# Two-step sorting with a turn across lanes in the planner of a max-plus layer

## The reference, cut to what matters

```
for a block of tokens xx:                      # all 16384 tokens
    t = max over d of (xx[:, d] + Wt[f, d])    # 256 d, 1024 f  -> t[token, f]
    z = t + bt; piecewise linear functions of z, mixed with gelu(x Wc) by a sigmoid gate, times Wd
```

## Time and profile before

| | |
|---|---|
| time, median of 3 runs (lowest, highest) | 6708.94 us (6705.71, 6711.29) |
| the profiled execution: time; span from its first to its last instruction | 6724.72 us; 6722.9 us |
| mean granted TensorE clock of the profiled execution | 0.959 of full speed |
| busy over the span: TensorE matmul, VectorE, ScalarE, GpSimd | 5978.2, 5148.0, 3296.8, 1789.5 us |

### The profile page before, as it was taken

The page is one execution under the profiler, slowest core; times in us unless marked ns, Lnnn a source line. Parts: engine busy times, 40 slices in busy tenths (PEclk is TensorE's granted clock), DMA queues, the critical chain, the costliest instruction groups (busy, mean ns, idle before and its releaser), DMA issues. The chain is left out here.

```text
span 6722.9 us, 104063 instructions
## 1 busy us (share of the span) xinstructions
PE 5978.2 (89%) x29554; PEld 4157.6 (62%) x29554; DVE 5148.0 (77%) x9496; ACT 3296.8 (49%) x6081; POOL 1789.5 (27%) x3698
## 2 busy tenths in 40 slices
PE   9998999999988884699999996876675999999999
PEld 6667999999977773466666664544443444444444
DVE  8993333333358888799999998998785999999998
ACT  6662222222234442466666664221122877787777
POOL 3330000000014442465656564247463000000000
PEclk9999999999989997899999998998887999999999
DMA  4440000000024442222121221246354222212221
GB/s 137 134 131 18 0 0 0 0 0 0 0 81 151 154 154 94 82 71 75 70 75 70 75 73 57 67 142 221 136 199 159 67 82 79 79 67 81 77 80 49
DMA packets 366380, 552.30 MB, mean 82 GB/s; under 512 B 29264, under 2 KB 299216, under 8 KB 366288
## 3 DMA queue, kind: packets, MB, share of 16 engines
q1 hardware_dynamic: 322944, 400.58, 18.2%
q0 software_dynamic: 43344, 150.64, 6.6%
HBM read 310.46 MB, written 240.67 MB: 82 GB/s over the span
## 5 line engine op out<-in xcount | busy, mean ns | idle before, releaser
L1710 PE MATMUL t_fetched<-t_wpart,t_onehot 128*128 128x512 f32 x4096 | 1221.6, 420 | 35.7 <-DVE t_tout L1815 15.5
L1815 DVE SCALAR_TENSOR_TENSOR t_tout<-t_fetched,t_top,t_tout 128x1024 f32<-128x1024 f32 x896 | 1149.3, 1283 | 35.5 <-PE t_fetched L1710 4.5
L580 PEld LDWEIGHTS l_ps<-hx,l_whh 128*128 128x128 f32 x8192 | 962.7, 193 | 16.8 <-DVE hx L521 3.7
L580 PE MATMUL l_ps<-hx,l_whh 128*128 (+1 forms) x8192 | 950.7, 275 | 3.2 <-DVE hx L521 3.2
L1710 PEld LDWEIGHTS t_fetched<-t_wpart,t_onehot 128*128 128x128 f32 x4096 | 690.7, 188 | 269.4 <-DVE t_tout L1815 131.0
L2112 PE MATMUL ts_fetched<-t_wpart,ts_onehot 128*128 128x512 f32 x2008 | 632.7, 450 | 209.2 <-ACT ts_onehot L2087 82.4
L545 ACT ACTIVATE l_act<-l_ps 128x128 f32<-128x128 f32 x1024 | 283.6, 277 | 1055.0 <-PE l_ps L580 1055.0
L2606 DVE SCALAR_TENSOR_TENSOR f_line<-f_hinge,f_vec,f_line 128x1024 f32<-128x1024 f32 x512 | 656.8, 1283 | 50.6 <-ACT f_hinge L2490 36.2
L2112 PEld LDWEIGHTS ts_fetched<-t_wpart,ts_onehot 128*128 128x128 f32 x2008 | 380.8, 207 | 397.8 <-DVE ts_tout L2180 232.6
L512 DVE TENSOR_TENSOR l_ig<-l_act 128x128 f32<-128x128 f32 x256 | 74.8, 292 | 592.3 <-ACT l_act L545 592.3
L2540 PE MATMUL f_pso<-f_fused,f_wd 128*128 128x512 f32 x1024 | 469.6, 602 | 36.8 <-DVE f_fused L2593 36.8
(11 more groups left out here) (379 smaller groups left out, 10666.6 us busy)
## 6 DMA issues: line engine op xcount, KB each, us to landing
t<-t_tout SPq DMA_DIRECT2D x128, 512.0 KB, 2.6
f_t<-t SPq DMA_DIRECT2D x64, 1024.0 KB, 5.2
g_adj<-in_adj SPq DMA_DIRECT2D x128, 256.0 KB, 3.0
g_adjt<-in_adjt SPq DMA_DIRECT2D x128, 256.0 KB, 2.8
t_x<-x_normalised SPq DMA_DIRECT2D x130, 128.0 KB, 2.3
g_x<-in_x SPq DMA_DIRECT2D x64, 256.0 KB, 2.8
x_kept<-g_x SPq DMA_DIRECT2D x64, 256.0 KB, 2.2
g_x<-x_kept SPq DMA_DIRECT2D x64, 256.0 KB, 2.8
```

The lines of the kernel that those rows point to most:

```text
L580: mm = pe.matmul(ps_g[s][q][:, c2, r, :], w_hh[:, k, row:row + P], hx[:, k, ds(t, 1), :].rearrange("p o b -> p (o b)"), start=False, stop= ...
L1710: mm = pe.matmul(fetched[c % RING][:, h * CH:(h + 1) * CH], one_hot[g][:, c % GRP * P:(c % GRP + 1) * P], w_part[part][:, k, h * CH:(h + 1 ...
L1815: dve.scalar_tensor_tensor(t_out[j][:, :], column[:, :], value, t_out[j][:, :], ALU.add, ALU.max)\
```

## The change

`tropical_plan` alone is changed. (1) The key holds the token's full number: 32768 x open + token + 1, where token + 1 = 128 x (tile + 1) + lane - 127. (2) Each lane sorts its two lists as before, in 16 rounds. (3) TensorE then multiplies the sorted keys with 32 stretches of a doubled identity matrix: the keys of rank r go to the lane that lies 4 x (r mod 32) places further round. In each matmul 8 columns move (four ranks of two halves). (4) VectorE copies the result out of PSUM, counts `above` from it as before, and sorts a second time in 16 rounds. (5) The row number is now read from the key, and the spare rows from a small table, so that a few instructions that made it from tile and lane go.

```diff
+OPEN_ONE = 32768.0
+TURNS = 32
...
         @block.tensor
         def _(pe):
+            pe.wait_ge(ident2_ready, 1)
+            pe.wait_ge(lanes_sorted, 1)
+            by_turn = [t[:, :, :].rearrange("p k (r m) -> p m k r", m=TURNS) for t in (sorted_key, ps_turned)]
+            for m in range(TURNS):
+                mm = pe.matmul(by_turn[1][:, m, :, :], ident2[:, m * (P // TURNS):m * (P // TURNS) + P],
+                               by_turn[0][:, m, :, :], start=True, stop=True)
+            mm.then_inc(lanes_turned, 1)
             pe.wait_ge(counted, 1)
...
+            def descending(src, between):
+                for r in range(TILES // 8):
+                    eight = slice(8 * r, 8 * r + 8)
+                    for k in range(KD):
+                        last = dve.max(sorted_key[:, k, eight], src[:, k, :])
+                    then(last)
+                    for k in range(KD):
+                        last = dve.match_replace(left_key[:, k, :], sorted_key[:, k, eight], src[:, k, :], -1.0)
+                    then(last)
+                    src = left_key
+                    if r == 0:
+                        between()
+
+            def turnable():
+                for r in range(2):
+                    last = dve.tensor_copy(ident2[:, r * P:(r + 1) * P], ident[:, :])
+                last.then_inc(ident2_ready, 1)
+                for r in range(3):
+                    last = dve.tensor_scalar(spare_row[:, r:r + 1], v["p_plus"][:, :], float(TOK + r * P + 1), None, ALU.add)
+                then(last)
...
+            dve.tensor_scalar(token_no[:, :], v["tile_no"][:, 0:TILES], float(P), v["p_plus"][:, :], ALU.mult, ALU.add)
             then(dve.tensor_scalar(key[:, :, :], done_count[:, :].rearrange("p (s k) -> p k s", k=KD),
-                                   -2.0 * P, 2.0 * P * P, ALU.mult, ALU.add))
+                                   -OPEN_ONE, OPEN_ONE * P - (P - 1), ALU.mult, ALU.add))
...
+            descending(key, turnable)
+            dve.sem_inc(lanes_sorted, 1)
+
+            dve.wait_ge(lanes_turned, 1)
+            then(dve.tensor_copy(key[:, :, :], ps_turned[:, :, :]))
             for c, g in enumerate(CLASSES[1:] + (0, CLASSES[0])):
-                last = dve.tensor_scalar(above[:, KD * c:KD * c + KD, :], key[:, :, :], 2.0 * P * (g + 1), None, ALU.is_ge)
+                last = dve.tensor_scalar(above[:, KD * c:KD * c + KD, :], key[:, :, :], OPEN_ONE * (g + 1), None, ALU.is_ge)
             then(last)
             dve.tensor_reduce(count[:, :], above[:, :, :], AX.X, ALU.add).then_inc(counted, 1)
-
-            src = key
...
+            descending(key, find_most)
...
-            dve.tensor_scalar(row[:, :, :], order[:, :, :], -1.0, float(P), ALU.add, ALU.mult)
+            dve.tensor_scalar(no_token[:, :, :], order[:, :, :], 0.0, spare_row[:, 0:1], ALU.is_equal, ALU.mult)
...
-            then(dve.tensor_scalar(row[:, :, :], row[:, :, :], v["p_plus"][:, :], None, ALU.add))
-            then(dve.tensor_tensor(from_row[:, :, :], row[:, :, :], no_token[:, :, :], ALU.add))
-            then(dve.tensor_tensor(row[:, :, :], row[:, :, :], no_token2[:, :, :], ALU.add))
+            dve.scalar_tensor_tensor(from_row[:, :, :], order[:, :, :], -1.0, no_token[:, :, :], ALU.add, ALU.add)
+            then(dve.scalar_tensor_tensor(row[:, :, :], order[:, :, :], -1.0, no_token2[:, :, :], ALU.add, ALU.add))
```

More of the change, by code:

```diff
@@ L1871, in tropical_plan @@
         ps_most = ctx.enter_context(nc.psum_tensor("tp_psmost", [1, C], F32))
+        ps_turned = ctx.enter_context(nc.psum_tensor("tp_psturned", [P, KD, TILES], F32))
         done_count, rows, ident = (v[n] for n in ("done_count", "rows", "ident"))
@@ L1874, in tropical_plan @@
             sem(n) for n in ("counted", "count_turned", "most_ready", "most_turned"))
+        ident2_ready, lanes_sorted, lanes_turned = (sem(n) for n in ("ident2_ready", "lanes_sorted", "lanes_turned"))
         steps = Steps(sem("steps"), 1)
@@ new lines, in turnable, with find_most @@
+            def turnable():
[5 more added lines that the diff above has]
+                then(last)
+            def find_most():
+                dve.wait_ge(count_turned, 1)
+                dve.tensor_reduce(most[:, :], ps_count[:, :], AX.X, ALU.max).then_inc(most_ready, 1)
@@ L1891, in _ @@
             steps.begin(0)
+            dve.tensor_scalar(token_no[:, :], v["tile_no"][:, 0:TILES], float(P), v["p_plus"][:, :], ALU.mult, ALU.add)
             then(dve.tensor_scalar(key[:, :, :], done_count[:, :].rearrange("p (s k) -> p k s", k=KD),
-                                   -2.0 * P, 2.0 * P * P, ALU.mult, ALU.add))
+                                   -OPEN_ONE, OPEN_ONE * P - (P - 1), ALU.mult, ALU.add))
             for k in range(KD):
-                last = dve.tensor_tensor(key[:, k, :], key[:, k, :], v["tile_no"][:, 0:TILES], ALU.add)
+                last = dve.tensor_tensor(key[:, k, :], key[:, k, :], token_no[:, :], ALU.add)
@@ L1917, in _ @@
-            then(dve.tensor_scalar(whole[:, :, :], sorted_key[:, :, :], 0.5 / P, -0.25, ALU.mult, ALU.add))
+            descending(key, find_most)
+            then(dve.tensor_scalar(whole[:, :, :], sorted_key[:, :, :], 1.0 / OPEN_ONE, -0.25, ALU.mult, ALU.add))
             then(dve.tensor_scalar(whole[:, :, :], whole[:, :, :], ROUND, None, ALU.add))
             then(dve.tensor_scalar(whole[:, :, :], whole[:, :, :], ROUND, None, ALU.subtract))
-            dve.tensor_scalar(is_open[:, :, :], sorted_key[:, :, :], 2.0 * P, None, ALU.is_ge)
@@ L1921, in _ @@
-            then(dve.scalar_tensor_tensor(whole[:, :, :], whole[:, :, :], -2.0 * P, sorted_key[:, :, :], ALU.mult, ALU.add))
+            dve.tensor_scalar(is_open[:, :, :], sorted_key[:, :, :], OPEN_ONE, None, ALU.is_ge)
+            then(dve.scalar_tensor_tensor(whole[:, :, :], whole[:, :, :], -OPEN_ONE, sorted_key[:, :, :], ALU.mult, ALU.add))
             then(dve.memset(order[:, :, TILES:SLOTS], 0.0))
             then(dve.tensor_tensor(order[:, :, 0:TILES], whole[:, :, :], is_open[:, :, :], ALU.mult))
-            dve.tensor_scalar(row[:, :, :], order[:, :, :], -1.0, float(P), ALU.add, ALU.mult)
+            dve.tensor_scalar(no_token[:, :, :], order[:, :, :], 0.0, spare_row[:, 0:1], ALU.is_equal, ALU.mult)
@@ L1932, in _ @@
-            then(dve.tensor_tensor(from_row[:, :, :], row[:, :, :], no_token[:, :, :], ALU.add))
-            then(dve.tensor_tensor(row[:, :, :], row[:, :, :], no_token2[:, :, :], ALU.add))
+                last = dve.tensor_scalar(no_token2[:, :, :].rearrange("p k (s r) -> p (k s) r", r=2)[:, :, r],
+                                         order[:, :, :].rearrange("p k (s r) -> p (k s) r", r=2)[:, :, r],
+                                         0.0, spare_row[:, 1 + r:2 + r], ALU.is_equal, ALU.mult)
```

5 lines of the change are left out of this document (1 added, 4 removed).

## The result

| | before | after |
|---|---|---|
| time, median of 4 runs beside each other | 6709.6 us (6705.71 to 6711.29) | 6601.5 us (6599.79 to 6602.89) |
| profiled execution, its own time | 6724.7 us | 6602.1 us |
| ratio, 95% interval | | 0.984 (0.9828 to 0.9853) |

The account below looks back on a forecast made before the run. VectorE bounds the plan and sets the pace in slots of 16 to 3; no engine is full over all slots. Plan +27.5 and slots -162.0 give -134.5 us, so 6708.9 becomes 6574 us, range 6558 to 6598.

Parts of the forecast that it names:

- The start of each half stays: Slots stage: the start of each half costs the same as before; no term in the sum.
- the other stages ... see the same data: Outside plan and slots: only those two can move, the other stages and the 44 us general round see the same data.
- the turn: Plan: 32 float32 matmuls on TensorE, fully exposed, 32 x 0.22 + 0.4 = +7.4 us, bounds 3.8 and 13.4.
- The number of slots: Slots: host calculation of turned lists gives 106 slots and 402 uses instead of 128 and 502, saving 162.0 us.
- The price of a slot: Slots: prices stay, from 22.95 us for 16 candidates to 4.65 us for 2.
- The rest of the plan: Plan: sort +18.9, small copies and adds +1.0, PSUM copy +0.9, row numbers -0.7; whole plan +27.5 us (19 to 36).
- each saved slot only relieves GpSimd's queue: Slots: each slot left out takes its three indirect DMAs off GpSimd's queue, so nothing is put behind anything.
- The gathers: Slots of 2, 3, 4: repeated places stretch DMA by f; 4% for 6598 to 6695 us, 1% no change, 2% slower.
- 273 f - 416: Slots of 2, 3, 4: extra us if DMA time stretches by f; eats the 134.5 us saving at f = 2.0.
- rival 2: Slots: lists don't shrink, so the plan's +27.5 us stands alone, 6736 us; chance 3%.
- the balance was not near perfect: Slots: judges a rival where slots follow the means over lanes, saving 246 us, so 6490 us; chance 2%.
- The rule on small matmuls: Plan: by the skill's some 25 ns a matmul the 32 would take 0.8 us; the forecast preferred the trace's weight loads.

Follow-up runs that it names:

- Experiment 2: Changed kernel with all 32 matmuls on the identity's first 128 columns, so no key leaves its lane: 6754.1 us, 1.0067 of the kernel before.
- experiment 1: Kernel before, unedited, run again; its profile is the second profile of before: 6708.3 us, 1.0001, profiled at 6713.6.
- experiment 11: Kernel before with 128 one-element VectorE memsets ahead of the plan, on the chip where before took 6723.3 us: 6724.9 us, 1.0004.
- experiment 9: Changed kernel with keys split into two fp32r parts moved by one matmul, plus 23 memsets, first chip: 6600.5 us, 0.9816 of the kernel before.
- experiment 10: Changed kernel with keys in two fp32r parts and 23 memsets, run on a second chip: 6589.2 us, 0.982 of the kernel before.
- experiment 13: Changed kernel with 74 matmuls of the identity on TensorE ahead of the turn: 6614.6 us, 0.9839 of the kernel before.
- experiment 5: Changed kernel with ten more slots of 2, on spare rows, in each half: 6682.6 us, 0.9958 of the kernel before.
- experiment 12: Changed kernel with 4 turns instead of 32, four matmuls of 64 columns: 6623.0 us, 0.9853 of the kernel before.
- experiment 4: Kernel before with 101 one-element VectorE memsets ahead of the plan: 6723.4 us, 1.0022 of the kernel before.
- experiment 6: Changed kernel with 26 VectorE memsets ahead of the plan: 6593.2 us, 0.9824 of the kernel before.
- experiment 7: Changed kernel with 64 VectorE memsets ahead of the plan: 6609.0 us, 0.9849 of the kernel before.
- experiment 15: Changed kernel with 26 VectorE memsets again, on a chip where the kernel before takes 6710.5 us: 6594.7 us, 0.9828.
- experiment 3: Kernel before with 32 extra TensorE matmuls behind the plan's transposes: 6708.4 us, 0.9999 of the kernel before.

## Why the prediction was right in kind and 26 us off in size

The steps that failed: "The start of each half stays" (12.5 us), "the other stages ... see the same data" (8.0 us), both terms put at nothing, and the turn at 7.4 us instead of 13.8 (6.4 us). Any one of them is more than the 3.5 us by which the time left the range. By the prediction's own steps, with the misses against 134.5:

- **The number of slots**: right in all twelve classes (x402, 106, 72, 14). Experiment 2 shows that the turn and nothing else of the change brings the saving. The host's calculation, tied to the twelve numbers of before, was the step that carried the forecast.
- **The price of a slot**: held within 2% from 16 down to 3, where VectorE sets the pace. In the class of 2 the forecast took 4.65 us from a profile that held pauses (experiments 1 and 11). Since only 6 of those slots went, this costs less than 2 us. The slots as a whole gave 165.8 instead of 162.0, -3.8 on the miss.
- **The turn**: the step "32 matmuls ... 32 x 0.22 + 0.4 = +7.4" is the mis-sized term. It took 13.79 us, above the upper bound of 13.4, because each float32 call is two instructions; experiments 9 and 10 show it from the other side, with 32 instructions in 6.97 us. The duration of one was right, at the clock of 0.50 that the turn had (experiment 13). The evidence stood in the rows I quoted: L1131 has x16, and the source behind it calls 8. I read them as 16 calls. +6.4.
- **The rest of the plan**: second sort 18.9 for 18.9, copy 0.42 for a share of 0.9; with the turn set aside the plan came 0.5 us under the forecast. The recorded lower bound of 19 us for the plan is too low: its terms' own lower bounds add to 22.7.
- **"The start of each half stays"**, and the claim that each saved slot only relieves GpSimd's queue: wrong. The forecast had a cost for each slot and none for the end of a block. The two gaps with drains in them grew by 12.5 us in the marks (6.3 + 6.2). Experiments 2, 5 and 12 tie their length to the number of slots alone, with turned and unturned lists, and old and new code. Had the blocks ended at 80 and 46 slots they would not have grown; by the runs it was chance that they did.
- **"The other stages ... see the same data"**: true, and not enough. The last stage took 8.0 us more with the same data and the same loop, since VectorE's code ahead of it is longer. Experiments 4, 6, 7, 11 and 15 show this; TensorE's code does not do it (experiment 3). The queue of instructions moves one packet in each of the change's five pauses.

That is 6.4 - 0.5 + 12.5 + 8.0 - 3.8 + 0.4 = 23.0, from -134.5 to -111.5. The other 3.4 us, to -108.1, lie between the two profiled executions and their medians.

**The rivals.** The gathers did not become the bound: the DMA share of the class of 2 is 0.73, against 0.72 in the second profile of before, and the slot stayed at 4.4 us. (The recorded sum 273 f - 416 holds only from f = 1.97 on; below 1.6 only the slots of 2 would have grown, by 195 f - 279.) The lists shrank (rival 2 is what experiment 2 built, 6754 rather than 6736, the difference being turn, pauses and spread), and the balance was not near perfect. What hit the forecast was none of them but the turn, counted at half, and two costs in stretches that it had left out.

**The rule on small matmuls.** By an estimate from the Trainium skill ("TensorE: Matmul & The Clock Gate", Back-to-back issue gap), 32 times some 25 ns, the turn would have been 0.8 us; that section of the Trainium skill gives the figure for a lone matmul, without a budget for its weight load. The trace has 13.79, 0.215 an instruction at a clock of 0.50. With 64 moving columns instead of 8 an instruction took 0.243 (experiment 12): with a full weight load for each, the weight sets nearly all of the pace, not the moving columns.

**What stays open.** What GpSimd does in its drain, and by what law it falls back; why the pauses end at 127 and 128 added instructions; and why TensorE and ScalarE pause in the slots of 2 on one chip and in the first profile of before.

## What to carry to other kernels

A list that waits for its fullest lane can be balanced by a sort, a shift by rank and a sort again, and what that yields can be computed beforehand to the slot, if the same arithmetic first reproduces the counts of the trace. Compare the number of instructions in a group with the number of calls in the source before a duration is multiplied: float32 matmuls appear twice. Give the end of a block a price of its own: here it changed with the number of slots. And where a change adds instructions to an engine, look at that engine's "issue" waits in later, unchanged loops, and at the packets of the instruction queue there; moving the code by a few dozen instructions gave back 9 us here.

## What the runs showed of the hardware

- **GpSimd's drain behind a block of indirect DMAs** depends on how many slots (three such DMAs each) it held, not on what they moved: 36 slots 9.447 us, 46 2.913, 48 3.403, 70 8.797, 74 0.957, 80 2.427. From 46 to 48, from 48 to 70 and from 74 to 80 it grows by 0.245 us a slot. Between 36 and 46 and between 70 and 74 it falls back; the values would fit a sawtooth of some 36 slots, which these six points do not prove. No DMA engine moves anything from 4712 to 4720, inside one of them.
- **A loop's time depends on where its code lies**: five pauses of about 3 us, with one packet of the instruction queue in each, and half as many instruction packets again (52 to 78), switched on by 101 one-value memsets over 1000 us earlier and off by 27 more. Sixty-four instructions more on TensorE did nothing.
- **A float32 matmul** of 128x128 weights and 8 columns is two instructions of 0.215 us each at a clock of 0.50, and 0.11 at 1.00; as fp32r it is one of 0.218 with 16 columns, at 0.50.
- **The clock** was 0.50 after a rest of 5.15 us that followed 15 us of work, and fell from 1.00 to 0.50 some 2.2 us into a busy run of 64 matmuls of 8 columns, which followed such work after 1.07 us. In the change it stayed at 0.50 through 13.79 us of such matmuls.
